# Ping-ponged feed-forward parameters, separate load semaphores, and token-shift transfers issued from ScalarE's queue

## What is computed

```python
xn = layernorm(x)
s  = recurrence(xn)                      # u = gelu(..)*sigmoid(..); s_t = A s + B u; y = C s + D
t  = xn
for i in range(6):                       # DEPTH
    t = attn_layer(shift_tokens(t), Wqkv[i], q_scale[i], k_scale[i], Wo[i]) + t
    t = ffn_layer(shift_tokens(t), ln_g[i], ln_b[i], W1[i], b1[i], W2[i], b2[i]) + t
out = x + s * silu(t)

def shift_tokens(t):                     # second half of the features comes from the token before
    a, s = split(t, 2, -1)
    return concat([a, pad(s, one zero token in front)[:, :-1]], -1)

def ffn_layer(x, g, bln, W1, b1, W2, b2):
    xn = (x - mean(x)) / sqrt(var(x) + 1e-5) * g + bln
    a, gate = split(xn @ W1 + b1, 2, -1)           # 2 x 341 columns
    return a * gelu(gate) @ W2 + b2
```

## Time and profile before

| what | value |
|---|---|
| device time, 3 runs | 1736.51, 1739.27 (median), 1743.57 us |
| the profiled execution | 1741.98 us, its span 1740.2 us |
| TensorE busy | 1666.1 us (96% of the span) |
| VectorE busy | 1381.5 us (79%) |
| GpSimd busy | 1187.3 us (68%) |
| ScalarE busy | 1092.9 us (63%) |
| granted TensorE clock, mean | 0.985 of full |
| chain that ended last | TensorE 89%, VectorE 4%, all DMA issue and landing 4% |

### The profile page before, as it was taken

The page is one execution under the profiler, slowest core; times in us unless marked ns, Lnnn a source line. Parts: engine busy times, 40 slices in busy tenths (PEclk is TensorE's granted clock), DMA queues, the critical chain, the costliest instruction groups (busy, mean ns, idle before and its releaser), DMA issues.

```text
span 1740.2 us, 74075 instructions
## 1 busy us (share of the span) xinstructions
PE 1666.1 (96%) x31420; PEld 1210.5 (70%) x31420; DVE 1381.5 (79%) x2661; ACT 1092.9 (63%) x1943; POOL 1187.3 (68%) x1163
## 2 busy tenths in 40 slices
PE   5889999999999999999999999999999999999995
PEld 2357777777777777677777677777677777677774
DVE  4688888887888888788888788888788887788863
ACT  2256666666666666566666566666666666566653
POOL 0377777776777767676776677677677777666751
PEclk9799999999999999999999999999999999999998
DMA  3032223332223323222323222333222332222222
GB/s 106 25 93 66 68 67 79 89 76 71 66 68 81 88 68 78 68 65 69 96 71 78 70 68 63 92 78 77 71 69 66 80 87 74 74 64 66 66 61 76
DMA packets 109735, 127.86 MB, mean 73 GB/s; under 512 B 52064, under 2 KB 55648, under 8 KB 109152
## 3 DMA queue, kind: packets, MB, share of 16 engines
q1 hardware_dynamic: 109408, 123.13, 27.9%
HBM read 20.27 MB, written 2.10 MB: 13 GB/s over the span
## 4 chain that ended last, share of the span: by engine, by line
PE 89%; DVE 4%; SPq 2%; ACT 2%; DMA 2%; issue 1%; POOL 0%; ACTq 0%; DVEq 0%; POOLq 0%
PE QKb L471 21%; PE O L594 11%; PE F L499 9%; PE VTb L512 9%; PE S L471 9%; PE S L529 8%; PE S L559 5%; PE F L616 4%; PE F L628 4%; PE F L629 3%; PE S L522 2%; SPq L397 1%; DVE t L823 1%; PE F L568 1%; DMA prm<-in_params 1%
## 5 line engine op out<-in xcount | busy, mean ns | idle before, releaser
L968 POOL TENSOR_TENSOR t<-t 128x512 f32<-128x512 f32 x384 | 488.7, 1273 | 306.6 <-DVE t L823 298.7
L823 DVE TENSOR_TENSOR t<-QKb,table 128x1024 f32<-128x1024 f32 x384 | 468.8, 1221 | 156.8 <-ACT sq L668 156.3
L962 POOL TENSOR_TENSOR t<-t,rn 128x512 f32<-128x512 f32 x384 | 400.5, 1043 | 136.0 <-DVE rn L863 136.0
L471 PE MATMUL QKb<-wq_sb,x_sh 128*128 128x512 f32 x768 | 426.3, 637 | 12.4 <-DVE t L823 11.7
L668 ACT ACTIVATE sq<-QKb 128x512 f32<-128x512 f32 x384 | 230.8, 601 | 321.7 <-PE QKb L471 314.7
L499 PEld LDWEIGHTS F<-wo_sb,OT 128*128 128x128 f32 x1536 | 202.9, 193 | 89.6 <-issue 88.7
L512 PEld LDWEIGHTS VTb<-cst,t 128*128 128x128 f32 x1536 | 186.6, 141 | 104.8 <-issue 94.0
L512 PE MATMUL VTb<-cst,t 128*128 128x128 f32 x1536 | 230.6, 273 | 0.6 <-POOL t L962 0.5
L594 PEld LDWEIGHTS O<-PT,V 64*64 64x64 f32 x12288 | 199.2, 135 | 42.7 <-issue 41.8
L876 DVE TENSOR_REDUCE ss<-sq 128x16 f32<-128x1024 f32 x192 | 224.4, 1169 | 0.0
L594 PE MATMUL O<-PT,V 64*64 64x32 f32 x12288 | 219.2, 221 | 0.9 <-DVE rn L863 0.5
(11 more groups left out here) (136 smaller groups left out, 2165.9 us busy)
## 6 DMA issues: line engine op xcount, KB each, us to landing
V<-v_tok SPq DMA_DIRECT2D x1440, 64.0 KB, 2.0
wq_sb<-in_wqkv SPq DMA_DIRECT2D x36, 256.0 KB, 3.7
wo_sb<-in_wo SPq DMA_DIRECT2D x6, 512.0 KB, 5.0
xs<-xm SPq DMA_DIRECT2D x48, 64.0 KB
xs<-xm SPq DMA_DIRECT2D x48, 63.5 KB
w_sb<-in_w SPq DMA_DIRECT2D x6, 341.0 KB, 3.3
w_sb<-in_w SPq DMA_DIRECT2D x6, 192.0 KB, 3.1
y_spill<-OT SPq DMA_DIRECT2D x1, 1024.0 KB, 4.1
```

The costliest lines, as they stand in the source:

```text
L471: return pe.matmul(out_, x_sh[:, pr, P * tile:P * (tile + 1)], wq_sb[:, col:col + 512], start=True, stop=True)
L823: dve.tensor_tensor(t12[:, v, :, :].rearrange("p c (h d) -> p c h d", h=8), QK_ps.rearrange("p (h d) -> p h d", h=8).unsqueeze(1) .to_broa ...
L962: pool.tensor_tensor(w, w, rn[:, vv // 4, 8 * (vv % 4):8 * (vv % 4 + 1)].unsqueeze(2) .to_broadcast([P, 8, DH]), ALU.mult).then_inc(qk_nor ...
L968: pool.tensor_tensor(w, w, t12[:, v, 1, :].rearrange("p (h c d) -> p h c d", h=8, c=2)[:, :, ::-1, :], ALU.add).then_inc(add_done, 1)
```

## The change

- The one semaphore in_ffn becomes three: in_w1, in_w2, in_prm. TensorE now waits for W1 before the W1 products, for W2 before the W2 products, and ScalarE for the parameters before L713.
- prm has two halves, used by layers in turn. Counted from the start of the last step of the old layer, as load_layer does, the parameters of the next layer are issued in slot 2 instead of slot 38; W1 is issued in slot 34, W2 in slot 36.
- The three transfers of the token shift are taken from SyncE and issued from ScalarE's queue, in slot 0 between the PT copy and the OT copy.
- Order: the exponential goes behind the copy of the transposed tile on ScalarE; the softmax sums go behind the sum of squares on VectorE; F_END goes from 37 to 36; two more pieces on TensorE and two on ScalarE are written in another order.

```diff
-F_W1, F_GEL, F_HID, F_W2, F_END = 32, 32, 33, 35, 37
+F_W1, F_GEL, F_HID, F_W2, F_END = 32, 32, 33, 35, 36
-        prm = sb("prm", [P, R_ALL])
+        prm = sb("prm", [P, 2, R_ALL])
-        in_wo, in_ffn = sem("in_wo"), sem("in_ffn")
+        in_wo, in_w1, in_w2, in_prm = sem("in_wo"), sem("in_w1"), sem("in_w2"), sem("in_prm")
@@ sync: load_layer
-                if slot == F_END + 1:
-
-                    wait(sp, ff_final, l * B)
-                    sp.dma_start(w1_sb[:, :], w1[l]).then_inc(in_ffn, 16)
-                    sp.dma_start(w2_sb[:, :, :], w2[l])\
-                      .then_inc(in_ffn, 16)
-                    sp.dma_start(prm[:, :], params[l]).then_inc(in_ffn, 16)
+                if slot == 2:
+
+                    wait(sp, ff_final, (l - 1) * B)
+                    sp.dma_start(prm[:, l % 2, :], params[l]).then_inc(in_prm, 16)
+                if slot == F_HID + 1:
+
+                    wait(sp, w1_ready, l * B * NCH)
+                    sp.dma_start(w1_sb[:, :], w1[l]).then_inc(in_w1, 16)
+                if slot == F_W2 + 1:
+
+                    wait(sp, w2_ready, l * B)
+                    sp.dma_start(w2_sb[:, :, :], w2[l]).then_inc(in_w2, 16)
@@ sync: step
-                    f, pr = batch(s, par, v, F_SH)
-                    if f is not None:
-
-                        wait(sp, mid_done, f + 1)
-                        wait(sp, normed, f * NT)
-                        sp.dma_start(xs[:, :, 0:D // 2], xm[:, pr, :, 0:D // 2]).then_inc(xs_moved, 16)
-                        sp.dma_start(xs[1:P, :, D // 2:D], xm[0:P - 1, pr, :, D // 2:D]).then_inc(xs_moved, 16)
-                        sp.dma_start(xs[0:1, 1:NT, D // 2:D], xm[P - 1:P, pr, 0:NT - 1, D // 2:D]).then_inc(xs_moved, 16)
@@ tensor: step
-                        if pr == 0:
-                            wait(pe, in_ffn, (f // B + 1) * 48)
+                        if f % B == 0:
+                            wait(pe, in_w1, (f // B + 1) * 16)
...
                     f, pr = batch(s, par, v, F_W2)
                     if f is not None:
+                        if f % B == 0:
+                            wait(pe, in_w2, (f // B + 1) * 16)
@@ scalar: step
-                    a, k, st, pr = quad(s, par, v, L_EXP)
-                    if live(a, QUADS):
-                        wait(act, sub_done, a + 1)
-                        act.activation(E[:, k, :], E[:, k, :], ACT.Exp).then_inc(exp_done, 1)
                     u, vv, st, pr = unit(s, par, v, L_TR)
...
+                    a, k, st, pr = quad(s, par, v, L_EXP)
+                    if live(a, QUADS):
+                        wait(act, sub_done, a + 1)
+                        act.activation(E[:, k, :], E[:, k, :], ACT.Exp).then_inc(exp_done, 1)
...
+                        if f % B == 0:
+                            wait(act, in_prm, (f // B + 1) * 16)
...
                     a, k, st, pr = quad(s, par, v, L_PT)
                     if live(a, QUADS):
                         wait(act, pt_ready, a + 1)
                         wait(act, o_ready, a - 1)
                         act.copy(PT[:, k % 2, :, :].rearrange("p c q -> p (c q)"), PT_ps).then_inc(pt_evac, 1)
...
+                    f, pr = batch(s, par, v, F_SH)
+                    if f is not None:
+
+                        wait(act, mid_done, f + 1)
+                        wait(act, normed, f * NT)
+                        act.dma_start(xs[:, :, 0:D // 2], xm[:, pr, :, 0:D // 2]).then_inc(xs_moved, 16)
+                        act.dma_start(xs[1:P, :, D // 2:D], xm[0:P - 1, pr, :, D // 2:D]).then_inc(xs_moved, 16)
+                        act.dma_start(xs[0:1, 1:NT, D // 2:D], xm[P - 1:P, pr, 0:NT - 1, D // 2:D]).then_inc(xs_moved, 16)
```

More of the change, by code:

```diff
@@ L331, in _ @@
             sp.dma_start(wo_sb[:, :, :], wo[0]).then_inc(in_wo, 16)
[L332 to L334 removed]
+            sp.dma_start(w1_sb[:, :], w1[0]).then_inc(in_w1, 16)
+            sp.dma_start(w2_sb[:, :, :], w2[0]).then_inc(in_w2, 16)
+            sp.dma_start(prm[:, 0, :], params[0]).then_inc(in_prm, 16)
             def load_layer(s, v, b_):
@@ L551, in step @@
                         mm.then_inc(tx_ready, 1)
+                    f, pr = batch(s, par, v, F_XT)
+                    if f is not None:
+                        wait(pe, normed, (f + 1) * NT)
+                        wait(pe, ff_final, f)
+                        wait(pe, x_staged, staged(s, v))
+                        for t in range(NT):
+                            mm = pe.transpose(BANK_XT[:, P * t:P * (t + 1)], xn[:, t, :], ident)
+                        mm.then_inc(xnT_ready, 1)
                     a, k, st, pr = quad(s, par, v, L_PT)
@@ L560, in step @@
                         mm.then_inc(pt_ready, 1)
-                    f, pr = batch(s, par, v, F_XT)
-                    if f is not None:
-                        wait(pe, normed, (f + 1) * NT)
-                        wait(pe, ff_final, f)
-                        wait(pe, x_staged, staged(s, v))
-                        for t in range(NT):
-                            mm = pe.transpose(BANK_XT[:, P * t:P * (t + 1)], xn[:, t, :], ident)
-                        mm.then_inc(xnT_ready, 1)
                     f, pr = batch(s, par, v, F_HID)
@@ L698, in step @@
                         stage(BANK_TX[:, 0:N], 1 - par)
+                    f, pr = batch(s, par, v, F_HID)
+                    if f is not None:
+                        gelus(f, pr, [2])
+                    f, pr = batch(s, par, v, F_AFF)
+                    if f is not None:
+                        if f % B == 0:
+                            wait(act, in_prm, (f // B + 1) * 16)
+                        wait(act, xnT_ready, f + 1)
+                        wait(act, w1_ready, f * NCH)
+                        act.activation(xc[:, :], BANK_XT[:, 0:N], ACT.Identity, bias=prm[:, f // B % 2, R_B:R_B + 1],
+                                       scale=prm[:, f // B % 2, R_G:R_G + 1]).then_inc(xn_done, 1)
                     a, k, st, pr = quad(s, par, v, L_PT)
@@ L703, in step @@
                         act.copy(PT[:, k % 2, :, :].rearrange("p c q -> p (c q)"), PT_ps).then_inc(pt_evac, 1)
-                    f, pr = batch(s, par, v, F_HID)
+                    f, pr = batch(s, par, v, F_SH)
                     if f is not None:
-                        gelus(f, pr, [2])
-                    f, pr = batch(s, par, v, F_AFF)
-                    if f is not None:
-                        if pr == 0:
-                            wait(act, in_ffn, (f // B + 1) * 48)
-                        wait(act, xnT_ready, f + 1)
-                        wait(act, w1_ready, f * NCH)
-                        act.activation(xc[:, :], BANK_XT[:, 0:N], ACT.Identity, bias=prm[:, R_B:R_B + 1],
-                                       scale=prm[:, R_G:R_G + 1]).then_inc(xn_done, 1)
+                        wait(act, mid_done, f + 1)
[3 more added lines that the diff above has]
+                        act.dma_start(xs[0:1, 1:NT, D // 2:D], xm[P - 1:P, pr, 0:NT - 1, D // 2:D]).then_inc(xs_moved, 16)
                     a, k, st, pr = quad(s, par, v, L_PV)
@@ L864, in step @@
                                                      op1=ALU.mult).then_inc(nw_seq, 1)
+                    u, vv, st, pr = unit(s, par, v, L_SS)
+                    if live(u, UNITS) and vv % 2 == 0:
+                        wait(dve, sq_done, u + 2)
+                        dve.tensor_reduce(ss[:, vv // 4, 8 * (vv % 4):8 * (vv % 4) + 16],
+                                          sq[:, vv % 4:vv % 4 + 2, :].rearrange("p a (h d) -> p (a h) d", h=8),
+                                          AX_X, ALU.add).then_inc(ss_done, 1)
                     a, k, st, pr = quad(s, par, v, L_EXP)
@@ L872, in step @@
                         dve.reciprocal(rs[:, k, :], sm[:, k, :]).then_inc(rs_done, 1)
-                    u, vv, st, pr = unit(s, par, v, L_SS)
-                    if live(u, UNITS) and vv % 2 == 0:
-                        wait(dve, sq_done, u + 2)
-                        dve.tensor_reduce(ss[:, vv // 4, 8 * (vv % 4):8 * (vv % 4) + 16],
-                                          sq[:, vv % 4:vv % 4 + 2, :].rearrange("p a (h d) -> p (a h) d", h=8),
-                                          AX_X, ALU.add).then_inc(ss_done, 1)
                     f, pr = batch(s, par, v, F_ST)
```

7 lines of the change are left out of this document (2 added, 5 removed).

## The result

The changed kernel takes 1970.65 us (median of 4 runs, 1969.81 to 1976.48), the kernel before on the same chip 1741.03 us: the ratio is 1.133, with a 95% interval of 1.130 to 1.136. The profiled execution took 1976.48 us, its span is 1974.7 us, and the mean granted clock of TensorE has gone from 0.985 to 0.93. TensorE is busy for 1767.9 us (90% of the span) where it was 1666.1 us (96%), with the same number of matmuls.

What follows compares the result with a forecast made beforehand. TensorE's own work was taken to bound steady steps. 1742.0 - 21.0 (layer ends) + 194 (45 x 4.3 us for idle time and clock) = 1915, less 2.7 us to the median of the runs: 1912 us, range 1740 to 1990 us.

Steps and rivals of the forecast that it cites:

- The bound: Steady steps: only TensorE's work counts, busy 33.34 of 33.35 us; rearranging the other engines can gain nothing.
- The layer ends, 21.0 us: Five steps ending a layer: ScalarE's wait for the parameters goes, nothing else is late, the whole 21.0 us gained.
- The three issues, 4.2 us: ScalarE's queue, slot 0: three shift transfers occupy it 4.2 us, as on SyncE; the OT copy starts 3.6 us late.
- TensorE's idle time, 3.1 us: TensorE before L471: 2.8 us idle in slot 2, the rest lost at the next L471, 3.1 us a step.
- The clock, 1.2 us a step: TensorE after its idle time: clock falls in two of three steps at 1.9 us, counted as 1.2 us a step.
- case C: The forecast case: ScalarE's queue held by the three issues, 1840 to 1997 us, and what lies down to B; chance 0.73.
- A: ScalarE's queue hands transfers over in some 0.1 us each; only the layer ends count, 1718 us; chance 0.10.
- B: Third issue on ScalarE costs its floor, 1.9 us for all three: 1752 or 1734 us, to 1770 us; chance 0.12.
- D: Dearer still: two queues hold each other up at one DMA engine, or clock stays low longer; above 1997 us; chance 0.05.
- E: Layer ends keep their stall because another load is late: 21 us more, 1933 us; 1 in 10, no own case.

Runs made afterwards that it cites:

- SyncE held: The changed kernel with one more wait: SyncE starts no V move of slot 0 before that step's shift has landed; 1901.66 us, ratio 1.095.

## Why the prediction was right, and where its sizes were off

The measured time lies inside the range, near its upper end, and the mechanism is the one forecast. The sum was 59 us short, nearly all of it in the term of the clock.

*The bound.* Right: nothing that was rearranged on the other engines changed a step of 33.35 us (the order alone: ratio 1.0007).

*The layer ends, 21.0 us.* Right. 1741.98 - 21.0 = 1721 us against the kernel's own time, or 1718 us by the median; with the shift on SyncE the kernels took 1715.9 and 1718.0 us, and nothing else was late there.

*The three issues, 4.2 us.* Right in kind: the block is the third issue and comes from the transfer ahead of it. The size was 5.3 us: 3.8 us for the third in place of 2.7. I had named the V moves as a reason for 0.7 us more and left them out of the sum; they make 1.1 us. The other way, the queue got to the first issue 0.46 us ahead of the PT copy and not 0.03 us behind it, so the OT copy came 4.2 us late and not 3.6.

*TensorE's idle time, 3.1 us.* Measured: 3.16 us in the mean of nine steps. That the numbers agree is partly luck. I had put 2.8 us into slot 2 and 0.3 us at the L471 of slot 3; all of the 3.16 us lies before the L468 of slot 2 (28.43 us in the nine steps). A second loss exists, but of 0.18 us and one place earlier, before the products with the values that stand ahead of that L471, and it shows only where the clock is at 1.00.

*The clock, 1.2 us a step.* This is the term that was mis-sized most: in its place TensorE was busy for 2.29 us more in the nine steps and 2.36 us in the mean of 43. I counted a fall in two of three steps at 1.9 us. It came in every one of the 43; 25 cost 1.9 us of busy time and 18 cost 3.0 us, as the layer end with 3.3 us of idle time had the earlier trace rows, while I had priced it by the two cheaper ones. About 0.35 us of this is not the clock (0.35 us at full clock with more matmuls, 0.35 to 0.55 us with SyncE held), and I had set down such a cost, 0.4 us beyond the idle time for a step without a fall, and left it out of the steps without one. That the rest is the clock is shown by the run with more matmuls: with the clock at 1.00 its busy time per step is 33.34 us, the added 2.6 us and 0.35 us. The lower end of the range, 1840 us for this case, leaned on an idle time "too short for the clock to fall", about 2.4 us (2.7 less 0.3); with SyncE held it fell after 2.11 to 2.34 us.

Together 5.45 us a step in those nine and 5.59 us in the mean of 43, in place of 4.3: 252 us in place of 194, and so 1970.65 us in place of 1912, inside the range of 1740 to 1990 us and inside case C.

*The rivals.* A (the issue is free) is wrong for three transfers, and its result holds for two: 1.36 us of issues on ScalarE's queue cost nothing in the steps, not because they are free but because they fit. Its limit, 1.05 us from a start at 610.7, was 1.5 us, since they start 0.49 us earlier than I had assumed (0.46 us ahead of the PT copy, not 0.03 us behind it). B is what the same instructions give in another order, 1746 us. What D names is at work: the other queue lengthens the issue by 1.1 us, and 18 of 43 steps pay for the clock as the dearest layer end had; the time stayed below D's 1997 us. E (a stall at the layer ends) is refuted. The Trainium skill, "DMA: Bandwidth & Descriptors", section "Issuing engines are not separate DMA queues", says that the time of issue "is usually small relative to the DMA itself". No row here has the landing of the large transfers, to be set against their 0.66 to 0.73 us; for the 256 bytes behind a transfer on one DMA engine it doesn't hold (3.8 us), and the measurement decides.

## What to carry to other kernels

Before transfers go to the queue of an engine that computes, read how long each holds the queue it is in now, and what stands ahead of it: a short transfer behind one that goes through a single DMA engine (127 partitions here; 112 did not) can hold the queue for microseconds, and with it every instruction of that engine behind it. The first remedy costs nothing in code: issue the short one first (225 us here), or leave it in the queue of an engine that computes nothing (250 us here). If TensorE bounds the kernel and must idle 2 us or more in each step, count slow matmuls in every step, at the price of the nearest row with the same idle time.

## What the runs showed of the hardware that was not expected

- The hold depends on the other queue: 2.76 us with SyncE quiet, 3.82 us with its V moves running (max 4.91 us).
- With 112 and 15 partitions in place of 127 the hold is gone at the median but not always: single issues still take up to 2.1 us.
- ScalarE's queue runs ahead of the engine: the first issue starts 0.46 us before the PT copy that stands ahead of it, so while the Gelu ahead of that is not done.
- More matmuls can make a kernel faster: 2.6 us of repeated work in each step gave 70 us.
- A fall of the clock came after idle times of 2.11 to 2.34 us in 38 of 43 steps of one kernel, and not after 2.10 and 2.48 us at single places of another. What decides between them stays open.
- In steps with an idle time of 0.9 to 3.0 us TensorE was also busy for 0.2 to 0.55 us longer than 33.34, with the clock at 1.00. Why stays open.
